# Last stage: gate and up biases folded into the expert weights, with the weights' last row subtracted as a plane

## The reference, cut to what matters

```python
d2 = sum(xs * xs) + sum(centroid * centroid) - 2.0 * (xs @ centroid.T)
w, sel = top_k(sqrt(max(d2, 1e-12)), 2);  w = softmax(w)
for e in range(8):
    h = silu(xs @ Wg[e] + bg[e]) * (xs @ W1[e] + b1[e])
    out = out + we[:, e:e + 1] * (h @ W2[e] + b2[e])
...
x = x + _layernorm(L3_ffn(_layernorm(x)))
```

## Time and profile before

| | us |
|---|---|
| median of 3 runs | 1178.87 |
| lowest and highest | 1174.91, 1188.52 |
| profiled execution, its own time | 1187.66 |
| its span in the trace | 1185.9 |
| mean granted TensorE clock | 0.902 of full speed |
| busy: PE, DVE, ACT, POOL | 955.9, 719.0, 572.6, 463.9 |

### The profile page before, as it was taken

How to read it: one execution, slowest core, us unless ns; L and a number is a source line. 1 busy time by engine, 2 the same in 40 slices (tenths; PEclk the granted TensorE clock), 3 DMA queues, 4 the chain that set the end, 5 groups by cost and what they waited for, 6 DMA issues and landing times. The chain is left out here.

```text
span 1185.9 us, 24279 instructions
## 1 busy us (share of the span) xinstructions
PE 955.9 (81%) x8086; PEld 754.2 (64%) x8101; DVE 719.0 (61%) x1952; ACT 572.6 (48%) x1193; POOL 463.9 (39%) x528
## 2 busy tenths in 40 slices
PE   6899884769993888897789999999997775139990
PEld 5566664769993655555666677767676654139990
DVE  4678645556665767773657666676635556735554
ACT  2577651325553466764444544454432533325552
POOL 1266664533444221211341333343443515733332
PEclk8899995779996999999999999999998887559995
DMA  8121110111212021111400101111113600111113
GB/s 283 49 66 50 50 52 10 35 43 43 55 45 76 26 68 56 56 57 40 139 19 2 32 9 37 38 37 38 38 38 91 237 2 18 33 40 49 53 44 107
DMA packets 80904, 67.05 MB, mean 57 GB/s; under 512 B 6753, under 2 KB 73592, under 8 KB 80402
## 3 DMA queue, kind: packets, MB, share of 16 engines
q1 hardware_dynamic: 76274, 57.04, 16.9%
q0 software_dynamic: 4512, 8.47, 2.2%
HBM read 39.30 MB, written 26.58 MB: 56 GB/s over the span
## 5 line engine op out<-in xcount | busy, mean ns | idle before, releaser
L454 DVE TENSOR_REDUCE a_rowmax<-a_banks 128x4 f32<-128x1024 f32 (+1 forms) x112 | 136.8, 1222 | 64.2 <-PE a_banks L721 28.1
L2314 POOL TENSOR_TENSOR a_both<-a_probs 128x512 f32<-128x512 f32 x64 | 86.2, 1347 | 159.9 <-ACT a_probs L2539 159.9
L576 ACT ACTIVATE a_probs<-a_banks 128x1024 f32<-128x1024 f32 x112 | 114.9, 1026 | 59.9 <-PE a_banks L707 47.2
L1207 POOL DMA_INDIRECT acc<-m_result,m_yb x77 | 75.5, 981 | 141.3 <-DVE m_result L1498 74.4
L2539 ACT ACTIVATE a_probs<-a_banks 128x1024 f32<-128x1024 f32 x64 | 65.6, 1025 | 88.5 <-PE a_banks L2598 88.5
L1607 ACT ACTIVATE m_gate<-m_banks 128x352 f32<-128x352 f32 (+1 forms) x93 | 42.9, 462 | 99.3 <-PE m_banks L1797 97.5
L2445 DVE TENSOR_REDUCE a_rowmax<-a_banks 128x4 f32<-128x1024 f32 x64 | 78.0, 1219 | 13.4 <-PE a_banks L2575 13.4
L1200 POOL DMA_INDIRECT rows<-m_yrow,m_idx x64 | 65.7, 1027 | 51.4 <-issue 21.8
L2612 PE MATMUL a_banks<-a_probs,a_V 128*64 128x256 f32 x512 | 69.4, 392 | 0.6 <-ACT a_craw L2528 0.6
L1478 DVE TENSOR_TENSOR m_h<-m_banks,m_gate 128x342 f32<-128x342 f32 (+1 forms) x55 | 28.5, 517 | 66.4 <-ACT m_gate L1607 59.9
L1820 PE MATMUL m_banks<-e_down,m_hT_hi 128*128 (+2 forms) x231 | 63.6, 344 | 1.0 <-DVE m_result L1498 1.0
(11 more groups left out here) (378 smaller groups left out, 2812.1 us busy)
## 6 DMA issues: line engine op xcount, KB each, us to landing
rows<-fill SPq DMA_DIRECT2D x16, 520.0 KB, 4.5
a_factor<-recip_rows SPq DMA_DIRECT2D x28, 256.0 KB, 4.8
rows<-fill SPq DMA_DIRECT2D x15, 455.0 KB, 4.2
m_yb<-rows SPq DMA_DIRECT2D x77, 65.0 KB, 1.8
f_expert<-in_experts SPq DMA_DIRECT2D x16, 257.5 KB, 2.9
m_parts<-acc SPq DMA_DIRECT2D x16, 256.0 KB, 4.9
bias<-in_bias_zero SPq DMA_DIRECT2D x1, 3248.0 KB, 20.7
e_gu_lo<-in_gu SPq DMA_DIRECT2D x1, 2736.0 KB
```

What stands on the lines that cost most here:

```text
L454: nc.vector.reduce_max(o, src, AX).then_inc(rowmax_ready, 1)
L576: nc.scalar.activation(probs[h][:, k, :, :], ps[:, 4:6, :], ACT.Exp, scale=SCALE).then_inc(exp_done, 1)
L1207: nc.gpsimd.indirect_dma_start(acc.rearrange("k n d -> (k n) d"), bass.IndirectOffsetOnAxis(yb[b % YB][:, P:P + 1].bitcast(U32), 0), resul ...
L2314: nc.gpsimd.tensor_tensor(both[u % 4][:, :, :], p[:, :, 0, :], p[:, :, 1, :], ALU.add).then_inc(both_ready, 1)
```

## The change

The gate and up biases are no longer added by matmuls. A token's last feature is replaced by the constant 1 in the rows that are sent to the experts (not in those that the router sees), the last row of each expert's gate and up weights is replaced by its bias, and the old last row is subtracted from the first 127 rows. For that, `load_last` fetches 127 rows of `e_gu_lo` from the weights and the row 127 from the biases, and a new tensor `last_row` (128 x 8 x 684), which holds the old last row in each of the first 127 partitions and zero in the last. GpSimd subtracts it (event `less_last`), for the experts 0 to 2 at the end of step 0 of `mixed_events`, 3 to 5 at the end of step 1, 6 and 7 at the end of step 2; ScalarE's split of an expert waits for it. The `bias` tensor keeps only the biases of the down part (128 x 1024).

```diff
+    else:
+        copies, bias_gu = biases
+        eng.dma_start(w["gu_lo"][0:P - 1, :, :].bitcast(F32),
+                      src_gu[0:n, 0:P - 1, :].rearrange("e p f -> p e f")).then_inc(w["loaded"], 16)
+        eng.dma_start(w["gu_lo"][P - 1:P, :, :].bitcast(F32), bias_gu).then_inc(w["loaded"], 16)
+        eng.dma_start(w["last_row"][:, :, :], copies.rearrange("p (e f) -> p e f", e=n)).then_inc(w["loaded"], 16)
...
+        w["last_row"] = sb("last_row", [P, n, width], F32)
-    w["parts"] = 16 + 16 * FC
+    w["parts"] = (16 if n < NE else 48) + 16 * FC
...
-BIAS = NE * (2 * F_EXP[3] + P)
+BIAS = NE * P
...
+    less_last = {0: [0, 1, 2], 1: [3, 4, 5], 2: [6, 7]}
...
-        events += [("split", e) for e in splits.get(k, [])]
+        events += [("split", e) for e in splits.get(k, [])] + [("less_last", e) for e in less_last.get(k, [])]
...
+                if kind == "less_last":
+                    pool.wait_ge(w["loaded"], w["parts"])
+                    raw_gu, _, _ = raw_parts(w, layer, r)
+                    nc.gpsimd.tensor_tensor(raw_gu, raw_gu, w["last_row"][:, r, :], ALU.subtract).then_inc(less_last, 1)
...
                 if by_distance:
+                    nc.vector.memset(yrow[1][:, :, P - 1:P], 1.0)
...
                 dve.wait_ge(router_ps, r + 1)
+                if by_distance:
+                    nc.vector.memset(yrow[0][:, tiles(r), P - 1:P], 1.0)
...
+                act.wait_ge(less_last, e + 1)
                 nc.scalar.activation(gu_hi, raw_gu, ACT.Copy)
...
-                    nc.scalar.activation(yrow[1][:, tiles(r), 0:P], yrow[0][:, tiles(r), 0:P], ACT.Copy).then_inc(copied, 1)
+                    n = P - 1 if by_distance else P
+                    nc.scalar.activation(yrow[1][:, tiles(r), 0:n], yrow[0][:, tiles(r), 0:n], ACT.Copy).then_inc(copied, 1)
...
-                    if by_distance:
-                        mm(o, bias_one[:, :], biases[:, e, s], start=False, stop=False)
...
-            load_experts(sp, 3, a["gu3"], a["down3"], w3)
+            load_experts(sp, 3, a["gu3"], a["down3"], w3, (a["gu_last"], a["bias_gu"]))
             sp.dma_start(g.bias[:, :].bitcast(F32), a["bias_zero"]).then_inc(g.bias_zeroed, 16)
```

More of the change, by code:

```diff
@@ L894, in _, with load_experts @@
                         busy(n, 0 if s == SEQS + 2 else 2)
-def load_experts(eng, layer, src_gu, src_down, w):
+def load_experts(eng, layer, src_gu, src_down, w, biases=None):
     n = ROUTED[layer]
@@ L907, in load_experts @@
             eng.dma_start(w["raw_down"][0:r, c, :], src_down[n, c * P:c * P + r, :]).then_inc(w["loaded"], 16)
-    eng.dma_start(w["gu_lo"][:, :, :].bitcast(F32), src_gu[0:n, :, :].rearrange("e p f -> p e f")).then_inc(w["loaded"], 16)
+    if biases is None:
+        eng.dma_start(w["gu_lo"][:, :, :].bitcast(F32), src_gu[0:n, :, :].rearrange("e p f -> p e f")).then_inc(w["loaded"], 16)
+    else:
[4 more added lines that the diff above has]
+        eng.dma_start(w["last_row"][:, :, :], copies.rearrange("p (e f) -> p e f", e=n)).then_inc(w["loaded"], 16)
     for c in range(FC):
@@ L1105, in experts @@
         if by_distance:
-            dist_ready, c2_ready, c2_ps, bias_loaded, bias_high, bias_low, bias_placed, stored = (st.sem(n) for n in (
-                "dist_ready", "c2_ready", "c2_ps", "bias_loaded", "bias_high", "bias_low", "bias_placed", "stored"))
+            dist_ready, c2_ready, c2_ps, bias_loaded, bias_high, bias_low, bias_placed, stored, less_last = (
+                st.sem(n) for n in ("dist_ready", "c2_ready", "c2_ps", "bias_loaded", "bias_high", "bias_low", "bias_placed",
+                                    "stored", "less_last"))
             (c_in_var, c_in_rstd, c_y_ready, c_yT_ps, c_yT_ready, c_qk_ps, c_qk_ready, c_v_ps, c_v_ready, c_z_ps,
@@ L1823, in down @@
                 if by_distance:
-                    last = mm(o[:, 0:P], bias_one[:, :], biases[:, e, 2 * width:2 * width + P], start=False, stop=True)
+                    last = mm(o[:, 0:P], bias_one[:, :], biases[:, e, :], start=False, stop=True)
                 last.then_inc(down_ps, 1)
@@ L2939, in packed @@
     a["moe3"] = np.hstack([t("L3_ffn_centroid"), iota])
-    a["bias3"] = np.hstack([f32("L3_ffn_bg"), f32("L3_ffn_b1"), f32("L3_ffn_b2")]).reshape(BIAS_ROWS, -1)
+    a["bias3"] = f32("L3_ffn_b2").reshape(BIAS_ROWS, -1)
+    a["bias_gu"] = np.hstack([f32("L3_ffn_bg"), f32("L3_ffn_b1")])[None]
+    a["gu_last"] = np.zeros((P, a["bias_gu"].size), np.float32)
+    a["gu_last"][0:P - 1] = a["gu3"][:, P - 1, :].reshape(1, -1)
     a["bias_zero"] = np.zeros((P, BIAS), np.float32)
```

## The result

| | before | after |
|---|---|---|
| median, us (4 runs each) | 1179.64 | 1283.61 |
| lowest and highest | 1174.91, 1188.52 | 1278.80, 1287.91 |
| profiled execution, its own time and its span | 1187.66, 1185.9 | 1281.49, 1279.6 |

The changed kernel takes 1.0871 times as long, with a 95% interval of 1.0793 to 1.0948. The forecast was 1272 with a range of 1256 to 1292; the time came 11.6 us above the forecast, inside the range.

The account below looks back on a forecast made before the run. PE was taken to bound the last stage's slots, with the loads before that stage deciding the outcome. The terms -12.2 + 104 + 0.5 + 0.6 = +92.9 us, from the median of 1178.9, gave 1272 us, range 1256 to 1292.

Parts of the forecast that it names:

- Part 2, the loads: End of ffn2: the 127-partition load runs on one DMA engine, so the last stage begins later, +104 us (+88 to +139).
- The rule that the prediction cited: Big load: a DMA uses as many engines as the largest number up to 16 dividing its slowest dimension; 127 gives one.
- Part 1, the removed matmuls: Last stage's slots: 2 of 8 gate_up matmuls go in each of 39 slots, 2.52 to 2.21 us a slot, -12.2 us.
- The second rival: Slots: removed matmuls give nothing back because another wait takes their place in each slot; 1284 us, chance 0.03.
- Part 3, the subtractions: Last stage before the slots: GpSimd's eight subtractions, 1.80 us each, fit its idle gaps; +0.5 us (0 to 14.4).
- Part 4, the memsets: VectorE: five one-column memsets, four in the router's chain, +0.6 us (0 to 1.8).
- The first: Rival on the big load: it is spread over several engines and the kernel gets a little faster, 1168 us, chance 0.07.
- The third: Rival on the big load: a lone engine takes 146 ns a run, +139 in place of +104, 1307 us, chance 0.03.
- the two small terms: The -12.2 us for removed matmuls in the slots and the +0.5 us for GpSimd's subtractions before them.

Follow-up runs that it names:

- experiment 8: Changed kernel with the 127 rows of the big load fetched as 124 and 3 partitions: 1217.07 us, ratio 1.0343 to the kernel before.
- experiment 9: Changed kernel with the 127 rows of the big load fetched as 112 and 15 partitions: 1185.18 us, ratio 1.0024 to the kernel before.
- experiment 1: Kernel before, with only its big load split into 127 partitions and one: 1280.33 us, ratio 1.0762.
- experiment 2: Changed kernel with the bias row packed into the weights in DRAM, so one DMA loads 128 partitions: 1187.15 us, ratio 0.9975 to the kernel before.
- experiment 4: Kernel of experiment 2, with TensorE reading the next block's expert number right behind the current gate_up: 1182.94 us, ratio 0.9939 to the kernel before.
- experiment 5: Kernel before, with only the expert's number read one slot early: 1179.48 us, ratio 1.0011.
- experiment 3: Kernel of experiment 2, with GpSimd only raising the semaphore and not subtracting: 1181.83 us, ratio 0.9928 to the kernel before.
- experiment 6: Kernel of experiment 2, with GpSimd's first three subtractions held until VectorE has written the second norm: 1177.92 us, ratio 1.0006 to the kernel before.
- experiment 7: Kernel of experiment 2, with each GpSimd subtraction cut into four pieces of 171 columns: 1173.33 us, ratio 0.9931 to the kernel before.

## Why the prediction was right, and what it had wrong

**Part 2, the loads: right in mechanism and in size.** The load ran on one engine, for the reason given and at the rate given (0.108 us a run, 0.109 taken). That the rate fitted so well is in part luck: it was carried over from 16 engines to one, and the same runs took 0.177 and 0.171 us in the loads of experiments 8 and 9. SP was through 132.4 us after the issue of the big load (1028.24 + 8.34 - 904.18), forecast 131.0; the zeros landed 13.5 us after their issue, 5.2 after SP was through, forecast 5.4. The barrier behind it took 1.0 us and not 2.8: before the change the 2.8 had been counted from GpSimd's last instruction, here SP was the last to come. The errors of +1.4 and -1.8 cancel. That this is the cause is shown by experiment 1, where the shape alone gives nearly all of the loss, and experiment 2, where all else gives none. The rule that the prediction cited from the Trainium skill ("DMA: Bandwidth & Descriptors", section "Why a DMA increments its semaphore by 16 and not by 1") gives four engines for 124 partitions and 16 for 112; the traces agree, with shares of 0.26 and 0.97 to 1.05 (experiments 8 and 9).

**Part 1, the removed matmuls: the mechanism right, the size off.** The term of -12.2 measured -7.1. The sum had asked which engine is late next, looked at VectorE's and ScalarE's slack, and found room. It didn't ask whether TensorE's own instruction stream had room: the 0.45 us for reading a block's expert were hidden behind queued matmuls and came out in every second slot. The second rival, "another wait takes their place", so held for some 40% of the gain. Experiments 4 and 5 show it.

**Part 3, the subtractions: the cover was right and the neighbour overlooked.** The term of 0.5 measured some 7. Their own time was 1.63 us each (1.80 taken), only the last took 2.08 beside VectorE's sum to x, and the gaps covered it. The step that failed is "hidden, so free": it treated an idle engine's time as the only cost. VectorE's instructions beside them waited. No row that the prediction used shows this, but the trace of the kernel before has it, in layer 0, where two instructions of a norm ran beside two operations of GpSimd and took 2.04 us; the same instruction with nothing beside it takes 0.33:

```profile
80.34 2.04 DVE L524 TENSOR_SCALAR a_f<-a_f,a_out_mv,a_out_rstd 128x128 f32<-128x128 f32 x2
80.16 1.22 POOL L360 TENSOR_SCALAR_AFFINE_SELECT a_probs<-a_probs 128x1024 f32<-128x1024 f32 x1 [1.64 <-ACT a_probs L576]
81.36 0.93 POOL L370 TENSOR_TENSOR e_gu_lo<-e_gu_lo,e_gu_hi 128x352 fp32r<-128x352 f32 x1
...
176.50 0.33 DVE L524 TENSOR_SCALAR a_f<-a_f,a_out_mv,a_out_rstd 128x128 f32<-128x128 f32 x1
```

The delay grows step by step: the third `m_c_in_rstd` starts 19.8 us after the stage begins in place of 17.9, the first `m_in_rstd` 32.0 in place of 28.6, the second 48.4 in place of 42.5, which is 5.9 us. Another 1.3 come behind it, where no subtraction runs: VectorE's `m_spot` waits 2.18 us for TensorE in place of 0.94. TensorE's granted clock is 0.55 there (from 1088.0 to 1090.6 us, mostly its level of 1.2 GHz), after three microseconds in which it was busy for 0.70 us; before the change it was 1.00 (2.4 GHz, 988.5 to 990.6). Whether the subtractions brought that about, by shifting TensorE's work, no run tells. Experiment 3 shows that the subtractions are the cost, experiments 6 and 7 that most of it comes by this wait. The Trainium skill ("GPSIMD Engine Reference", section "Specifications") states that GpSimd shares its SBUF interfaces with VectorE, in contention with VectorE instructions in a 2-port performance mode or with two SBUF inputs. Two of the delayed kinds have two tensors in SBUF, `m_cshift` and the sum to x; `m_cz`, with one tensor in PSUM, ran at 1082.98 in 0.42 us, its usual time, beside the last subtraction. The trace agrees so far, and `m_ctop`, a reduction of one tensor in SBUF, wasn't delayed either. That the norm's instruction and `m_cneg`, which have one tensor in SBUF, are delayed would be the performance mode's part; no run here tells that apart.

**Part 4, the memsets: nothing, as good as forecast** (0.6). Experiment 3 still has them, with a mixed part of 111.66 us.

**The rivals.** The first, a spread load, is refuted by the share of 0.06; what it said of the rest is experiment 2, and there the small gain came out at 0.25% and not 0.9%. The third, a slower lone engine at 0.146 us, is refuted by 0.108 us. The errors of the two small terms, +5.1 and +5.9, both went the same way, and together make 11.0 of the 11.6 us between forecast and result. That the time still lies in the range is luck as far as the +5.9 goes: the upper end was made for the second rival and the base's own spread, and both together left room for a cost that nobody had thought of.

## What to carry to other kernels

Before a load loses or gains a partition, factor the new number: the profile of before had its warning in a single stretch, a chunk of 86 partitions at a DMA share of 0.14, and padding or packing on the host keeps the 128. When matmuls are taken out of a loop that is bound by TensorE, ask for the room in its own instruction stream too, not only in the other engines. And an operation in an engine's idle time is free only if it leaves the neighbours alone: look at the lengths of what runs beside it, or cut it into pieces, or give it to the engine that would have waited.

## What was not expected of the hardware

- **A run's time depends on the shape of the DMA by more than its engines.** The same 2736-byte runs took 0.108 us in the load of 127 partitions, 2736 B / (404 / 16.5 GB/s) = 0.112 us in that of 128, but 0.177 us in the load of 124 (four engines) and, at 935 packets in 10 us on 16 engines, 0.171 us in that of 112 and 15. It isn't the number of engines, since both 1 and 16 can be fast and both 4 and 16 slow. What it is stays open; it wasn't tried further.
- **Some VectorE instructions wait for the end of a running GpSimd instruction**, they don't just run more slowly beside it: four that take 1.11 us alone took 5.07 us beside three of 1.63, and one of 0.16 us took 1.59. GpSimd waits for VectorE in the same way (2.08 us in place of 1.63). A reduction (0.42 us) and an addition with one tensor in PSUM (0.42 us) were not held up.
- **A small DMA behind a one-engine load holds SP for most of that load**: 101.31 us for a row of 21.4 KB, where the load's 1016 runs of 0.108 us make 110.
